# Attention keys: the own ones projected and turned a block earlier, the next context split and the rows normalised a block later

## The reference

```python
x = x + _L0_xattn_ref(_layernorm(x), ctx_2048, wq, wk, wv, wo, wk_ctx, wv_ctx, q_norm_w, k_norm_w)

# inside: 16 query heads, 4 key heads of 128, L = T = 256
q = rms_norm((x @ wq), q_norm_w)          # per head
k = rms_norm((x @ wk), k_norm_w);  v = x @ wv
k_ctx = rms_norm((ctx @ wk_ctx), k_norm_w);  v_ctx = ctx @ wv_ctx
q = q * cos + rotate_half(q) * sin;  k = k * cos + rotate_half(k) * sin      # not k_ctx
scores = q . concat(k_ctx, k) / sqrt(128) + causal mask over the own part
out = softmax(scores) @ concat(v_ctx, v);  return out @ wo
```

## Time and profile before

| what | us |
|---|---|
| median of 3 runs (1596.77 to 1601.76) | 1596.91 |
| the profiled execution's own time | 1596.18 |
| its span | 1594.9 |
| busy: PE, DVE, ACT, POOL | 1429.5, 1156.2, 975.1, 716.1 |
| attention stage, 0 to 905: span; PE busy | 905.00; 781.64 |
| batch of blocks 8 to 15, 159.62 to 266.17 | 106.55 |
| first batch from block 0, 27.44 to 159.62 | 132.18 |
| last batch, 798.25 to 905.00 | 106.75 |

### The profile page before, as it was taken

One profiled execution on the slowest core, in us unless ns is written; L12 is line 12 of the kernel. 1 busy time (PEld: TensorE's weight loads), 2 busy tenths in 40 slices (PEclk: granted clock), 3 DMA queues, 4 the chain that ended last, 5 costly groups with the idle time before them and its releaser, 6 DMA issues. The chain is left out here.

```text
span 1594.9 us, 24891 instructions
## 1 busy us (share of the span) xinstructions
PE 1429.5 (90%) x7820; PEld 1046.0 (66%) x7820; DVE 1156.2 (72%) x2836; ACT 975.1 (61%) x2647; POOL 716.1 (45%) x809
## 2 busy tenths in 40 slices
PE   7888989888979898889888789999998899999988
PEld 5665767666767676667676456666666566666653
DVE  5677776767767777777778875655566888888774
ACT  6565665666656656666565674555554666667655
POOL 5456464555554655655655600000003455555444
PEclk9789999999999999999998989999999999999999
DMA  7334555545545555555488998878885401111000
GB/s 282 70 83 118 119 126 115 114 113 124 125 120 114 125 115 117 115 123 126 106 203 202 255 308 276 287 248 256 267 264 161 151 21 47 54 54 41 28 14 27
DMA packets 321892, 223.76 MB, mean 140 GB/s; under 512 B 276960, under 2 KB 277088, under 8 KB 320352
## 3 DMA queue, kind: packets, MB, share of 16 engines
q1 hardware_dynamic: 321760, 222.16, 52.4%
HBM read 113.05 MB, written 41.94 MB: 97 GB/s over the span
## 5 line engine op out<-in xcount | busy, mean ns | idle before, releaser
L891 DVE SCALAR_TENSOR_TENSOR planes<-E,small,planes 128x384 f16<-128x384 f32 (+1 forms) x256 | 210.8, 843 | 70.5 <-POOL planes L1087 69.0
L1087 POOL TENSOR_SCALAR planes<-E,small 128x384 f16<-128x384 f32 (+1 forms) x256 | 160.0, 637 | 159.1 <-DVE small L912 151.7
L421 PE MATMUL bank<-wq,xT 128*128 128x512 f32 x768 | 199.6, 409 | 9.3 <-ACT wq L559 9.1
L687 ACT ACTIVATE E<-E,small 128x384 f32<-128x384 f32 (+1 forms) x256 | 170.8, 675 | 51.1 <-DVE small L904 51.0
L904 DVE CUSTOM_DVE_ANT_0 E<-quad,mask,small 128x384 f32<-128x384 f32 (+1 forms) x256 | 169.2, 677 | 44.7 <-PE quad L451 44.6
L1300 PE MATMUL bank<-wq,ot 128*128 128x512 f32 x768 | 187.6, 403 | 9.9 <-DMA ot<-ot_scratch 5.6
L479 PE MATMUL bank<-PT,vv 128*128 128x512 f16 x672 | 177.9, 401 | 0.0
L1300 PEld LDWEIGHTS bank<-wq,ot 128*128 128x128 f32 x768 | 147.8, 193 | 44.3 <-DMA ot<-ot_scratch 6.1
L421 PEld LDWEIGHTS bank<-wq,xT 128*128 128x128 f32 x768 | 143.4, 194 | 39.2 <-issue 9.3
L1080 POOL TENSOR_TENSOR t<-t 128x512 f32<-128x512 f32 x64 | 84.7, 1324 | 172.3 <-DVE t L878 172.3
L1596 POOL TENSOR_TENSOR cl<-cl,fixed 128x1 f32<-128x1 f32 x16 | 8.8, 550 | 279.5 <-DVE cl L1480 279.5
(11 more groups left out here) (313 smaller groups left out, 3304.1 us busy)
## 6 DMA issues: line engine op xcount, KB each, us to landing
...
```

The lines of the kernel that those rows point to most:

```text
L421: ins = pe.matmul(bQ[:], xT[p][:, k, qt * 128:qt * 128 + 128], wq[j][:, g, k, :], start=(part == 0 and k == 0), stop=(part == 2 and k == 3))
L687: act.activation(p, p, ACT.Exp, bias=nm[:, i % 2, h:h + 1], scale=-1.0, accum_out=sm[:, i % 2, h:h + 1]).then_inc(f["s_exp"], 1)
L891: dve.scalar_tensor_tensor(plane(i, 1, h), E[:, h, 0:width(i)], ri[:, i % 2, h:h + 1], plane(i, 0, h), ALU.mult, ALU.subtract).then_inc(f[ ...
L1087: pool.tensor_scalar(plane(i, 0, h), E[:, h, 0:width(i)], ri[:, i % 2, h:h + 1], 1.0, ALU.mult, ALU.mult).then_inc(f["p_n"], 1)
```

## The change

In the diff's order: own and context units change places, so that own units are the even ones, projected in even blocks; at the first group of a batch (bg % 4 == 0) the context's stays first, since the rows of the batch are turned only in block 6. The first batch keeps its first two units. The weight pieces of own and context change places likewise. Both units of a group are now transposed in the odd block: the own one, projected a block earlier, behind the scores, the context one inside P.V. Their ScalarE, VectorE and GpSimd steps move with them. In block 7 the own unit of the new batch is projected at the head of the block. The context's split moves from the end of block 4 into block 5; the loads of the rows move from block 4 to between block 5's transposes; the rows' statistics, normalisation, transposition and split all move to block 6, where P.V now comes before the transposition. The same sums are computed.

```diff
--- before.py
+++ after.py
@@ -125,18 +125,22 @@
     def unit(u):
 
 
-        bg, own = divmod(u, 2)
-        return bg, 1 - own if bg == 0 else own
+        bg, n = divmod(u, 2)
+        return bg, n if bg and bg % 4 == 0 else 1 - n
+
+    def own_before(u):
+
+        return sum(unit(w)[1] for w in range(u))
 
     def piece_of(p):
 
 
-        g, j = divmod(p, 4)
-        return g, (j + 1) % 4 if g == 0 else j
+        g, n = divmod(p, 4)
+        return g, ((1, 0, 2, 3) if g else (1, 2, 3, 0))[n]
 
     def pieces(g, j):
 
-        return 4 * g + (j - 1) % 4 + 1 if g == 0 else 4 * g + j + 1
+        return 4 * g + ((1, 0, 2, 3) if g else (1, 2, 3, 0)).index(j) + 1
 
     def piece(p):
 
@@ -314,7 +318,7 @@
         sp_w(0, "wkc")
         sp.dma_start(mask[:], a["mask"]).then_inc(f["mask_in"], 16)
         for g in range(1, 4):
-            for src in ("wkc", "wkv", "wq"):
+            for src in ("wkv", "wkc", "wq"):
                 sp_w(g, src)
         sp_c(2)
         sp_c(3)
@@ -330,14 +334,13 @@
                     for x in range(2):
                         sp_p_turn(i, half, x)
                         sp_last(i, 1 + 2 * half + x)
+                        if b + 1 < NB and r == 5 and half != x:
+                            sp_x(2 * b + 2 + half)
             elif i == NBLK:
                 sp_last(i, 4)
             if b + 1 < NB and r == 6:
                 sp_c(2 * b + 4)
                 sp_c(2 * b + 5)
-            if b + 1 < NB and r == 4:
-                sp_x(2 * b + 2)
-                sp_x(2 * b + 3)
 
 
 
@@ -495,22 +498,29 @@
 
     def pe_step(i):
         turn = i % 8 == 6 and i + 2 < NBLK
+        ahead = i % 8 == 7
+        if ahead:
+            pe_kv(i + 2, 0)
+            pe_kv(i + 2, 1)
         pe_s(i, 0)
         pe_s(i, 1)
         if i == 0:
             pe_q(1, 2)
-        pe_kv(i + 2, 0)
-        pe_kv(i + 2, 1)
+        if not ahead:
+            pe_kv(i + 2, 0)
+            pe_kv(i + 2, 1)
+        pe_s(i, 2)
+        pe_s(i, 3)
+        if i % 2:
+            pe_k_turn(i + 1)
         if turn:
+            for part in range(3):
+                pe_pv(i - 1, part)
             pe_x_turn(2 * (i // 8) + 2)
             pe_x_turn(2 * (i // 8) + 3)
-        pe_s(i, 2)
-        pe_s(i, 3)
-        if turn:
-            pe_pv(i - 1, 0)
-            pe_pv(i - 1, 1)
+            pe_scale(i)
         pe_q_turn(i + 1)
-        if scaled(i):
+        if scaled(i) and not turn:
             pe_scale(i)
         if i == 60:
             pe_w1_sum()
@@ -520,12 +530,10 @@
             ffn["pe_y"](0, 1)
         if not turn:
             pe_pv(i - 1, 0)
-            if i % 2 == 0:
-                pe_pv(i - 1, 1)
-        pe_k_turn(i + 2)
-        if i % 2:
+            if i % 2:
+                pe_k_turn(i + 2)
             pe_pv(i - 1, 1)
-        pe_pv(i - 1, 2)
+            pe_pv(i - 1, 2)
         if i == 62:
             pe.wait_ge(f["q_sq"], NBLK)
             ffn["pe_y"](0, 0)
@@ -562,7 +570,7 @@
         b, t = divmod(c, 2)
         sem, n = c_in(c)
         act.wait_ge(sem, n)
-        after(act, f["kv_mm"], 8 * b - 1)
+        after(act, f["kv_mm"], 8 * b)
         act.copy(cT[0][:, :, t * 128:t * 128 + 128],
                  stg[:, c % 2, :].rearrange("p (k n) -> p k n", k=4)).then_inc(f["c_hi"], 1)
 
@@ -589,12 +597,13 @@
             return
         act.wait_ge(f["kv_mm"], u + 1)
         after(act, f["kt_mm"], u)
+        after(act, f["k_rope"], own_before(u))
         act.copy(kn, kv4(u)[:, 0]).then_inc(f["k_raw"], 1)
 
     def act_k_scale(u):
         if u >= NU or not unit(u)[1]:
             return
-        act.wait_ge(f["k_rope"], u // 2 + 1)
+        act.wait_ge(f["k_rope"], own_before(u) + 1)
         act.wait_ge(f["n_rs"], u + 1)
         for t in range(2):
             ins = act.activation(ka[:, t], ka[:, t], ACT.Copy, scale=rs6[:, u % 2, t:t + 1])
@@ -656,7 +665,8 @@
         if u >= NU or unit(u)[1]:
             return
         act.wait_ge(f["n_rs"], u + 1)
-        after(act, f["kt_mm"], u)
+        after(act, f["k_rope"], own_before(u))
+        after(act, f["kt_mm"], u - unit(u - 1)[1])
         for t in range(2):
             ins = act.activation(kn[:, t], kv4(u)[:, 0, t], ACT.Copy, scale=rs6[:, u % 2, t:t + 1])
         ins.then_inc(f["k_n"], 1)
@@ -722,21 +732,30 @@
         if i == 0:
             act_w_hi(6)
         act_o(i - 2)
+        if i % 2 == 0 and i:
+            act_v_hi(i + 1)
         if i:
-            act_v_hi(i + 1)
             act_q_sq(i + 1)
         if 1 <= i <= 4:
             act_w_hi(2 * i + 6)
+        if i % 8 == 7:
+            act_k_raw(i + 2)
         act_exp(i, 0)
         act_exp(i, 1)
         if i == 0:
             act_q_sq(1)
-        act_k_raw(i + 2)
+        if i % 2:
+            act_k_scale(i + 1)
+        if i % 8 != 7:
+            act_k_raw(i + 2)
         act_k_sq(i + 2)
         act_ve(i + 2)
-        if turn:
-            act_x_hi(2 * (i // 8) + 2)
-            act_x_hi(2 * (i // 8) + 3)
+        if i % 8 == 5 and i + 3 < NBLK:
+            for m in (2 * (i // 8) + 2, 2 * (i // 8) + 3):
+                act_c_hi(m)
+                act_c_square(m)
+        if i % 2:
+            act_k_hi(i + 1)
         act_last(i, 0)
         act_exp(i, 2)
         act_k_n(i + 2)
@@ -745,18 +764,21 @@
             act_w_hi(7)
         elif i <= 4:
             act_w_hi(2 * i + 7)
+        if turn:
+            act_x_hi(2 * (i // 8) + 2)
+            act_x_hi(2 * (i // 8) + 3)
+        if i % 2:
+            act_v_hi(i + 1)
         act_q_hi(i + 1)
         if i == 0:
             act_v_hi(0)
             act_v_hi(1)
-        act_k_scale(i + 2)
-        act_k_hi(i + 2)
+        if i % 2:
+            if i % 8 == 7:
+                act_k_scale(i + 2)
+            act_k_hi(i + 2)
         if i in (1, 3):
             act_w_square(2 + i // 2)
-        if i % 8 == 4 and i + 4 < NBLK:
-            for m in (2 * (i // 8) + 2, 2 * (i // 8) + 3):
-                act_c_hi(m)
-                act_c_square(m)
         act_last(i, 1)
         act_last(i, 2)
 
@@ -947,35 +969,39 @@
             dve_w(5)
             dve_q(1)
         if turn:
+            dve_ln_a(2 * (i // 8) + 2)
+            dve_ln_a(2 * (i // 8) + 3)
+        dve_o_lo(i - 2)
+        if i % 2 == 0 and i:
+            dve_v_lo(i + 1)
+        dve_ri(i, 0)
+        if turn:
             dve_ln_b(2 * (i // 8) + 2)
             dve_ln_b(2 * (i // 8) + 3)
-        dve_o_lo(i - 2)
-        if i:
-            dve_v_lo(i + 1)
-        dve_ri(i, 0)
         if i == 0:
             dve_w(6)
         dve_last(i, 0)
         dve_ev(i, 2)
+        if i % 2:
+            dve_k_lo(i + 1)
+        dve_p_lo(i, 0)
+        dve_ev(i, 3)
+        dve_p_lo(i, 1)
+        if i % 2:
+            dve_v_lo(i + 1)
+        if 1 <= i <= 4:
+            dve_w(2 * i + 6)
+        dve_ri(i, 1)
         if turn:
             dve_x_lo(2 * (i // 8) + 2)
             dve_x_lo(2 * (i // 8) + 3)
-        dve_p_lo(i, 0)
-        dve_ev(i, 3)
         if scaled(i):
             dve_scale(i)
-        dve_p_lo(i, 1)
-        if 1 <= i <= 4:
-            dve_w(2 * i + 6)
-        dve_ri(i, 1)
         dve_q_lo(i + 1)
         if i == 0:
             dve_w(7)
         dve_p_lo(i, 2)
         dve_p_lo(i, 3)
-        if i % 8 == 5 and i + 3 < NBLK:
-            dve_ln_a(2 * (i // 8) + 2)
-            dve_ln_a(2 * (i // 8) + 3)
         if scaled(i):
             dve_unscale(i)
         if i == 0:
@@ -983,7 +1009,8 @@
             dve_v_lo(1)
         if 1 <= i <= 4:
             dve_w(2 * i + 7)
-        dve_k_lo(i + 2)
+        if i % 2:
+            dve_k_lo(i + 2)
         if i == 16:
             dve_co()
         dve_last(i, 1)
@@ -1061,8 +1088,7 @@
     def pool_k_rope(u):
         if u >= NU or not unit(u)[1]:
             return
-        pool.wait_ge(f["k_raw"], u // 2 + 1)
-        after(pool, f["k_rope"], u // 2)
+        pool.wait_ge(f["k_raw"], own_before(u) + 1)
         pool.tensor_tensor(kb[:, :, 0:64], kn[:, :, 64:128], tab[:, 3, :, 0:64], ALU.mult)
         pool.tensor_tensor(kb[:, :, 64:128], kn[:, :, 0:64], tab[:, 3, :, 64:128], ALU.mult)
         g_.did(pool.tensor_tensor(ka, kn, tab[:, 2, :, :], ALU.mult))
@@ -1105,24 +1131,33 @@
         pool.tensor_tensor(lo, loaded, hi.bitcast(F32), ALU.subtract).then_inc(f["wo_lo"], 1)
 
     def pool_step(i):
+        turn = i % 8 == 6 and i + 2 < NBLK
         pool_q_add(i + 1)
+        if i % 8 == 7:
+            pool_k_rope(i + 2)
         pool_norm(i, 0)
         pool_norm(i, 1)
-        pool_k_rope(i + 2)
+        if turn:
+            pool_ln_rs(2 * (i // 8) + 2)
+            pool_ln_rs(2 * (i // 8) + 3)
+        if i % 8 != 7:
+            pool_k_rope(i + 2)
         pool_rs(i + 2)
-        pool_k_add(i + 2)
-        if scaled(i):
+        if i % 8 == 7:
+            pool_k_add(i + 2)
+        if i % 8 == 5 and i + 3 < NBLK:
+            pool_c_lo(2 * (i // 8) + 2)
+            pool_c_lo(2 * (i // 8) + 3)
+        if scaled(i) and not turn:
```

(10 more changed lines are left out.)

## The result

| | before | after |
|---|---|---|
| median (range; 4 runs each) | 1598.06 (1596.77 to 1601.76) | 1634.83 (1631.32 to 1636.87) |
| ratio to before, 95% interval | | 1.0224 [1.0197, 1.0251] |
| the profiled execution; its span | 1596.18; 1594.9 | 1636.27; 1635.0 |
| from block 0 to block 8 | 132.18 | 140.45 |
| from block 8 to block 56 | 638.63 | 670.18 |

The kernel became 2.2% slower: 37 us on the medians, 40.1 on the profiled spans. I had forecast 1600, 4 us more than before, with a range of 1582 to 1616: the direction was right, and the size wrong by 36 us on the spans. The result lies above the range.

The account below looks back on a forecast made before the run. TensorE was taken to bound the attention stage, with 11 us of stalls in a 105.94 us batch. Seven batch changes at +1.1 (+8), first batch -2 and last -2 gave +4 on 1596.18: 1600 us, range 1582 to 1616.

Parts of the forecast that it names:

- block 7 near 14.5: Sign that the forecast holds: the block before a new batch lasts near 14.5 us, against 14.92.
- over 3 us of idle TensorE before q's turn: Sign in block 6: TensorE idles over 3 us before q's transpositions, ended by VectorE's low part of xT.
- Plain odd blocks: Blocks 1 and 3: a second chain through GpSimd's normalisation of heads 2 and 3 leaves only 0.14 us gain each.
- Plain even blocks: Blocks 0, 2, 4: one pair of transpositions fewer saves 0.25 us each, to 10.65; GpSimd's added rope stays hidden.
- Block 5: Context split and squares move in, delaying the key's high part: 16.0 us against 17.18, -1.2.
- Block 6: The turn: row steps lie open ahead of q, whose projection runs slow: 18.0 us, +5.3, between +3.6 and +7.
- Block 7: Own unit projected first; key turns 12.1 after the start, next block at 14.5 against 14.92: -0.4 us.
- Block 0: With the stall ahead of block 7's turn under 2 us, it may lose its slow stretch: -0.9 us on the mean.
- First batch: Even blocks no longer wait for q's weights' cast behind the keys' scaling: three times 0.6, -2 us.
- The last batch: It has no turn, so only the small gains: -2 us.
- Rival C: Dearer turn, q's projection wholly at half clock, second row tile late, plain odd blocks +0.3: 1614 us, chance 0.27.
- Rival A: Odd blocks drop to their floor because the second chain hides: 1557 us, with half of it 1578; chance 0.10.

Follow-up runs that it names:

- e2: The changed kernel with, in odd blocks, v's high and low parts behind q's, so the second reciprocal waits for its sum alone; 1617.05 us, ratio 1.0112.
- e3: e2 with the own keys' low part on VectorE moved behind the low part of head 1 in odd blocks; 1611.01 us, ratio 1.0067.
- e7: e6 with exp of head 3 ahead of the scaling of the context's keys on ScalarE in blocks 1 and 3; 1582.38 us, ratio 0.988.
- e11: e9 with the context key's low part ahead of those of heads 2 and 3 on VectorE in blocks 1 and 3; 1557.59 us, ratio 0.974.
- e1: The changed kernel with the context unit's keys transposed ahead of the scores in block 7, right after its projection; 1618.52 us, ratio 1.0124.
- e10: The whole change, turn included, with the edits of e1, e2, e3 and e8, and that of e7 in odd blocks; 1572.95 us, ratio 0.9825.
- e8: e7 with the low part of q's weights ahead of the low parts of heads 2 and 3 in blocks 2 and 4; 1576.57 us, ratio 0.9843.
- e6: The kernel before with only the keys' exchange, in blocks 0 to 3 of each batch, in the orders of e2 and e3; 1589.23 us, ratio 0.9923.
- e9: e8 with the rows' statistics, still in block 5, behind the last key's low part on VectorE; 1564.88 us, ratio 0.9771.

## Why the prediction was wrong

The spans differ by 40.1 us; I had said 4. Of the signs that I had named, block 7 near 14.5 did not come (16.46 by the count of the forecast), nor over 3 us of idle TensorE before q's turn; the others did. By the prediction's steps:

- **Plain odd blocks: right.** 13.49 forecast, 13.56 to 13.60 measured, by the chain that was walked. e2 shows that v's steps in front of the reciprocal held it, for 0.7 us. The key's low part moved as well (e3) gave a plain odd block nothing until exp of head 3 had moved too (e7).
- **Plain even blocks: right in length, wrong in clock.** Block 4 is 10.70 (10.65). Block 2 is 11.44 on the mean, since in half of the batches it ran slow right behind the odd block's wait. I had charged the clock at blocks 6 and 0 alone. +4.7.
- **Block 5: right in kind**, 16.46 against 16.0, above my 15.8 to 16.2. GpSimd's low parts beside VectorE, for which I had allowed 0.25, cost more: 1.51 us for a low part that takes 0.74 in block 35. +2.8.
- **Block 6: right on the mean** (20.98 less 3.0 is 18.0), with its parts another way. TensorE idles 1.34 to 2.85 before q's turn, not 3.3. Behind block 5's 4.68 us wait the context's projection ran slow in three of the seven turns (4.83, 4.67 and 4.81, in batches 0, 2 and 4; 3.02 in e11 at full clock) and a little slow in the other four (3.40 to 3.50). In the three, TensorE then idled 1.34 to 1.51 before q's turn and q's projection took 3.00 to 3.03; in the four it idled 2.68 to 2.85, and q's projection took 4.07, 4.15, 5.22 and 4.08 (at 259.03, 484.09, 707.04 and 818.73). So each turn paid at one place or the other, and that the mean of block 6 came out is partly luck. The rule of the Trainium skill ("TensorE: Matmul & The Clock Gate", HAM oscillation), that TensorE left idle between bursts runs the next one slow, holds as to the fall of the clock, but not that q's projection pays every time.
- **Block 7: wrong, the first failed step** ("by the same walk the key turns 12.1 after its start and the next block begins at 14.5"). Counted from its scores, as in the table, that was 11.5, and it took 13.46. I had walked rope, root, add and scaling from the projection, and had not asked what the raw copy in front of them waits for. That was the old unit's transposition, now behind the scores. 1.96 times 7 is 13.7 us; e1 shows it.
- **Block 0: wrong, hanging on that step** ("the stall ahead of that turn is then under 2 us, so block 0 may lose its slow stretch"). The stall was 3.80, and block 0 stayed at 11.50. 0.8 times 7 is 5.6. The step had a fault of its own too: in e1 the stall came down to 2.22 and block 0 only to 11.22 on the mean, in e10 to 2.09 and 11.34. So at most 0.4 of the 0.8 went with the stall; the rest was a term that I had mis-sized.
- **First batch: wrong** ("now gone from there: three times 0.6, -2"). +4.1 in blocks 0 to 4: block 2 rose by 3.6. There the wait for ScalarE's cast of q's weights fell as forecast (2.72 to 2.06), but behind it came a wait of 2.62 for the low part of the same weights. I had looked at which steps left the queue in front of the weights, not at what the steps left in it now wait for. e8 shows it.
- The last batch was right (-2.4 against -2). The start (+0.9) and what lies behind the attention (+1.8) were not forecast. From block 63 on, where the kernels are alike, the fourteen profiled executions take 695 to 701 us, so the 1.8 needs no cause in the change.

The misses add up: 13.7, 5.6, 6.1, 4.7, 2.8, 0.9, 1.8 and 1.4 of small ones are 37.0, against the 36.1 missing. The two that were steps of the walk (block 7 and the first batch) are 20 of them; 10 are the clock. Rival C had the sign but neither the place nor the size: it decides on q's projection over 5 us, which was so in one turn of seven. Its price and that of A count 27 odd blocks; the plain ones are 16, with block 5 they are 24. Rival A, the odd block at its floor, came only with other orders: 12.5 in e8 and 11.5 for block 1 in e11. The range failed because no case had the new waits of block 7 and of the first batch, nor a slow block 2, beside the turn.

Left open: why e10's first batch gains as much as it does, whether block 3 of e11 can lose its 0.62 us wait for the own keys, what decides which stretch runs slow, and what the orders of e6, e7 and e9 would give on the kernel before, with its units as they are.
